# The two stores of each group of v cover exactly the partitions that hold needed rows

## The reference, cut to what matters

```python
def _L1_gnn_ref(x, spatial_encoding, edge_encoding, Wq, Wk, Wv, Wo):
    n, d = x.shape                      # 3327, 128
    h = Wq.shape[0] // d                # 8
    q = (x @ Wq.T).reshape(d, n, h)
    k = (x @ Wk.T).reshape(d, n, h)
    v = (x @ Wv.T).reshape(d, n, h)
    a = jnp.einsum('dnh,dmh->dnm', q, k) * d ** (-0.5)
    a = jax.nn.softmax(a + spatial_encoding + edge_encoding, axis=2)
    out = jnp.einsum('dnm,dmh->dnh', a, v)
    return out.reshape(n, h * d) @ Wo.T
```

## Time and profile before

| what | us |
|---|---|
| median of three runs (11011.2 to 11017.62) | 11016.96 |
| the profiled execution | 11012.01 |
| its span from first to last instruction | 11010.2 |
| first store of the projection phase issued | 364.5 |
| first and last store of v issued | 388.1 and 596.6 |
| first DMA of the phase behind it issued | 605.3 |

### The profile page before, as it was taken

How to read it: one execution, slowest core, us unless ns; L and a number is a source line. 1 busy time by engine, 2 the same in 40 slices (tenths; PEclk the granted TensorE clock), 3 DMA queues, 4 the chain that set the end, 5 groups by cost and what they waited for, 6 DMA issues and landing times. The chain is left out here.

```text
span 11010.2 us, 306891 instructions
## 1 busy us (share of the span) xinstructions
PE 9969.5 (91%) x115286; PEld 4497.9 (41%) x115286; DVE 9811.3 (89%) x9374; ACT 10319.1 (94%) x7187; POOL 7991.1 (73%) x3346
## 2 busy tenths in 40 slices
PE   7769999999999999899999999998999999999988
PEld 7435533333333333333333333333333333333383
DVE  6669999999999999899999999998999999999958
ACT  6569999999999999999999999999999999999916
POOL 0048888888888888788888888887888888888800
PEclk9979999999999999999999999999999999999999
DMA  9887743333333333433323332334323333333264
GB/s 404 277 192 100 100 80 49 48 49 50 49 48 49 50 49 48 94 50 50 49 47 50 50 49 47 50 54 91 49 47 50 50 49 47 50 50 49 43 213 175
DMA packets 426704, 879.88 MB, mean 80 GB/s; under 512 B 86871, under 2 KB 349406, under 8 KB 381694
## 3 DMA queue, kind: packets, MB, share of 16 engines
q1 hardware_dynamic: 426588, 878.33, 40.1%
HBM read 722.35 MB, written 155.64 MB: 80 GB/s over the span
## 5 line engine op out<-in xcount | busy, mean ns | idle before, releaser
L1287 DVE SCALAR_TENSOR_TENSOR a_probs<-ps,adj_ring 128x1024 f32<-128x1024 f32 x7488 | 8859.1, 1220 | 752.0 <-PE ps L1175 630.1
L1259 POOL TENSOR_TENSOR a_pool_probs<-a_pool_probs,adj_ring 128x1024 f32<-128x1024 f32 x3328 | 7974.7, 2396 | 1861.1 <-ACT a_pool_probs L1245 1861.1
L1248 ACT ACTIVATE a_probs<-a_probs 128x2048 f32<-128x2048 f32 (+1 forms) x3328 | 8698.6, 2614 | 27.6 <-DVE a_probs L1287 27.2
L1245 ACT ACTIVATE a_pool_probs<-ps 128x1024 f32<-128x1024 f32 x3328 | 5008.3, 1505 | 44.6 <-PE ps L1175 44.3
L1175 PE MATMUL ps<-a_q,a_k 34*128 34x512 f32 (+1 forms) x21632 | 4087.6, 445 | 793.6 <-ACT a_pool_probs L1245 613.2
L1195 PE MATMUL ps<-a_probs,a_v 128*9 128x256 f32 x59904 | 3855.8, 380 | 0.0
L1175 PEld LDWEIGHTS ps<-a_q,a_k 34*128 34x128 f32 x21632 | 1792.1, 184 | 3463.4 <-ACT a_pool_probs L1245 1630.0
L1195 PEld LDWEIGHTS ps<-a_probs,a_v 128*9 128x9 f32 x59904 | 1578.5, 91 | 1598.6 <-issue 196.8
L1195 PE MATMUL ps<-a_pool_probs,a_v 128*9 128x256 f32 x26624 | 2065.6, 382 | 4.2 <-DMA a_v<-v_ext 2.7
L1195 PEld LDWEIGHTS ps<-a_pool_probs,a_v 128*9 128x9 f32 x26624 | 395.4, 88 | 974.7 <-issue 934.7
L682 POOL MEMSET v_rows<- 128x512 f32 x2 | 1.9, 1039 | 352.4 <-POOLq L94 352.4
(11 more groups left out here) (178 smaller groups left out, 2355.1 us busy)
## 6 DMA issues: line engine op xcount, KB each, us to landing
a_k<-k_parts SPq DMA_DIRECT2D x1664, 208.0 KB
a_q<-q_parts SPq DMA_DIRECT2D x3072, 16.0 KB
a_v<-v_ext SPq DMA_DIRECT2D x384, 117.0 KB, 2.1
adj_t<-tr SPq DMA_DIRECT2D x26, 1664.0 KB, 19.4
g2tile<-adj_t SPq DMA_DIRECT2D x26, 1664.0 KB, 7.1
nat<-in_adj SPq DMA_DIRECT2D x25, 1663.5 KB, 18.0
e_nat<-in_adj SPq DMA_DIRECT2D x25, 1663.5 KB, 6.9
adj_ring<-adj_t SPq DMA_DIRECT2D x54, 512.0 KB, 7.5
```

What stands on the lines that cost most here:

```text
L1245: nc.scalar.activation(probs(k), score(j), ACT.Exp, scale=SCALE).then_inc(scores_exped, 1)
L1248: nc.scalar.activation(sums_of(k), sums_of(k), ACT.Exp, scale=2.0).then_inc(sums_exped, 1)
L1259: nc.gpsimd.tensor_tensor(beside(c, probs(k)), beside(c, probs(k)), adj_of(c, j), ALU.mult).then_inc(multiplied, 1)
L1287: v.scalar_tensor_tensor(out=beside(c, probs(k)), in0=beside(c, score(j)), scalar=SCALE / 2, in1=adj_of(c, j), op0=ALU.mult, op1=ALU.add). ...
```

## The change

Two lines are replaced. For group g with columns `begin` to `end`, `upper` is now the number of partitions of the first store itself and `lower` the first partition of the second store itself. Before, the one was rounded up and the other down to a multiple of 16.

```diff
                     begin, end = v_groups[g]
-                    upper = min(P, -(-(P - begin // BLOCKS) // 16) * 16)
-                    lower = (P - end // BLOCKS) // 16 * 16
+                    upper = P - begin // BLOCKS
+                    lower = P - end // BLOCKS
                     sp.wait_ge(v_copied, HEADS * (g + 1))
                     sp.dma_start(v_ext[P:P + upper, begin:end], v_rows[g % 2][0:upper, 0:end - begin, :]
                                  ).then_inc(v_stored[g % 2], LOAD)
                     sp.dma_start(v_ext[lower:P, begin + 1:end + 1], v_rows[g % 2][lower:P, 0:end - begin, :]
                                  ).then_inc(v_stored[g % 2], LOAD)
```

## The result

| | before | changed |
|---|---|---|
| median of five runs | 11016.96 (11011.2 to 11018.31) | 11230.32 (11228.81 to 11239.62) |
| ratio | | 1.0195, 95% interval 1.0184 to 1.0206 |
| span of the profiled execution | 11010.2 | 11227.0 |
| projection phase, first store issued to first DMA behind it | 240.8 | 453.6 |

The kernel became 213 us slower while it stored 1.7 MB less. The slices show where, against the earlier trace rows: the second and third. The fourth to the sixth differ too, since work comes there that came 213 us sooner before.

A forecast was written before the change was run, and what follows sets the result against it. DMA engines bound the projection phase; on the fullest, 170.8 (q, k) + 275.8 (389 rows of v) + 3.2 (half rows) + 8 (landing, gaps) make 458 us, 217 over 240.8; on 11012 that is 11229 us, range 11180 to 11285.

The forecast's parts named there:

- The reading of three transfers: DMA dealing: equal shares over the most engines, up to sixteen, that the row count allows; read from 112, 15, 127 rows.
- SP's hold of 10.08 us: At the issue of the load of x: taken as a sign that its 127 rows lay on one engine.
- The share of 0.07 and the packets in single file: Load of x, 16.9 to 17.2 us: one engine of sixteen at work, 22 packets in 0.50 us, so 127 rows on one.
- The sum: Projection phase, fullest engine: 389 rows of v at 0.709 us plus q and k, 458 us in place of 240.8.
- The engine that never idles: Projection phase: the fullest engine's backlog covers the computing, the next group arriving some 5 us before it runs dry.
- Part 1: Stores of v at lines 623 and 625: 1.71 MB no longer stored gain 4 to 5 us if nothing else changes.
- the last rival: Whole kernel faster by over 22 us: no mechanism, as v's stores are 46 us per engine and lose 8% of bytes; 0.01.
- The 23.6 us left over: Phase before, 240.8 measured against 217.2 summed: landing, gaps and slower rows of v when sixteen engines store; 8 kept.
- Even dealing: Stores of v: rows dealt as evenly as the count allows, 0 us or 4 to 5 us gained, 11007 to 11012; chance 0.11.
- other engines: Stores of v: each one-engine store goes to another engine, 42 us fall away, 11187; chance 0.05.
- all on one: Stores of v: every count not a multiple of sixteen goes to one engine, 267 us on top, 11496; chance 0.06.
- the first rival: Stores of v dealt evenly, some engines one row more: 11007 to 11012, the change doing what its size suggests; chance 0.11.

The follow-up runs named there:

- e7_x_split: Kernel before, with the load of 127 rows of x taken as 112 and 15 rows, v's stores unchanged: 11021.02 us, ratio 1.0003.
- e6_split: Changed kernel's exact rows, each store cut into the largest multiple of 16 and a remainder in its own DMA: 11027.79 us, 1.0008 against the kernel before.
- e8_all_rows: Kernel before, with both stores of v covering all 128 partitions in every group: 11016.32 us, ratio 0.9998.
- e1: Kernel before, with only line 623 covering the exact counts, line 625 keeping multiples of 16: 129.6 us slower, ratio 1.0118.
- e2: Kernel before, with only line 625 covering the exact counts: 84.8 us slower, ratio 1.0077.
- e3: Kernel before, with only the stores of a prime count (109, 89, 19, 59) exact, the others multiples of 16: 165.5 us slower, ratio 1.0148.
- e5: Kernel before, with only group 1's row count at line 623 changed from 112: 109 rows 67.1 us slower, 122 34.4, 111 22.2, 110 5.1.

## Why the prediction was right

**The bound.** DMA bounds the phase: PE, DVE and ACT did the same busy time in both, and the phase grew by 212.8 of the 216.8 us of span.

**How rows are dealt.** The reading of three transfers (127 rows on one engine, 15 spread, 112 on sixteen) was confirmed: 109, 122, 111 and 110 in one place give 1, 2, 3 and 11 engines, primes and composites apart add up, and the rows under way show 13, 10, 14 and 3 engines for 39 and 78, 50, 98 and 69. The page of the Trainium skill named in the prediction (DMA: Bandwidth & Descriptors, "Why a DMA increments its semaphore by 16 and not by 1") gives the same rule, and the runs agree: shares of 0.06, 0.12 and 0.18 for one, two and three engines. That the engines used are the lowest-numbered is its statement; the runs show only that the 89 and the 59 rows share one.

One leg of the argument was wrong: SP's hold of 10.08 us at the load of x was given as a sign of the 127 rows. It stays with 112 rows (e7_x_split), so the count of 127 is not its cause; the load ahead is the likely one, not shown. The share of 0.07 and the packets in single file carried the step alone. Also, the 15 rows landed 1.7 us behind the 112 (10955.0 and 10953.3), not 1.3, which is the difference of the two durations; against the 7.5 us of work that 15 rows on one engine would be, it changes nothing.

**The sum.** Predicted for the phase 458 us, measured 453.6. A row alone on its engine took 0.69 us, not 0.709, 7 us less on 389 rows. The rest beside the packets: 453.6 - 170.8 - 389 x 0.69 - 3.2 = 11 us, where 8 was kept; 4 of the 11 are packets of q and k, which took 0.0495 us in place of 0.0483. The two misses offset each other in part. The median was forecast at 11229 and came at 11230.3, and that closeness is luck: it is 213 us over its own before, where 217 were forecast over a profiled execution 5 us below the median.

**The engine that never idles.** Right: the distances from group to group grew by 0.61 to 0.69 us per row more wherever 17 rows or more were added to the fullest engine, but for group 3 (9.4 us for 19 rows, 0.49), and compute hid nothing. Group 4 got 3.1 us faster with 50 and 98 rows in place of 64 and 112, on ten and fourteen engines: its rows took 0.93 us in the mean in place of 1.22.

**The bytes.** Part 1 was wrong as a term, without effect on the forecast. It priced 90 rows at 4 to 5 us "if nothing else changes". Storing the exact rows nearly evenly, with eleven DMAs more, was 10 us slower (e6_split), and storing 560 more cost nothing (e8_all_rows). The price took one rate for all rows, but rows of different stores have different rates. (Of the 19.3 MB of v, 1.71 are 9%, not the 8% of the last rival.)

**The 23.6 us left over.** The prediction put them down to landing, gaps and "rows of v that take longer when sixteen engines store at once". By the packets 19 of them are slow rows of v (62.6 us in place of 43.2) and 4 are packets of q and k at 0.0495 us in place of 0.0483; the packets overlap a little, which leaves room for landing and gaps. But the condition named is not the right one: in e8_all_rows sixteen engines store at once, and a row takes 0.71 us. It is stores of fewer than 128 partitions that have the slow rows. The forecast needed only that a row alone on its engine is not slow, and that held (0.69 us).

**The rivals.** Even dealing, other engines and all on one each failed at e1, e2, e3 or e5, by 20 us or more. The time that the first rival gave for the case that the change does what its size suggests, 11007 to 11012, was not reached either: with the rows spread by more DMAs it was 11028, 10 us above before. Spread rows without the added DMAs were not run.

**What would have shown it.** Predicted were a share of about 0.55 over the phase (0.50), stretches of some 75 and 100 us behind groups 1 and 2 (ACT's longest wait 98 us), and groups 3 and 4 nearly as before (9.4 us more, 3.1 less).

## What to carry to other kernels

Count a DMA's rows on its fullest engine before its bytes: with n rows, find the largest divisor of n up to 16 by trying 16, 15, 14 and so on (110 goes to 11 engines, which is easy to miss), and prefer a few unneeded rows to a prime count, or cut the transfer into a multiple of 16 and a rest. A row of 18 KB cost 0.64 to 0.74 us on the fullest engine here, and everything queued behind it on that engine waits with it, so 109 rows in place of 112 cost 67 us. When an issue is held, look at the transfers ahead of it first; when engines are busy, look at the rate too.

## What the runs showed of the hardware that was not expected

- Rows of 18 KB took an engine 0.71 us when both stores of a group covered all 128 partitions (windows of 413 to 422 GB/s) and 0.88 to 1.22 us in the mean when one or both covered fewer (windows of 223 to 340 GB/s, packets of q and k among them), at the same busy share of 1.0. 11.35 MB more were free (ratio 0.9998).
- A DMA of 89 rows on one engine, with 59 behind it on the same one, held SP not at its own issue (0.25 us) but at the three behind it: 15.31, 43.65 and 49.48 us.
- With compute idle for 30 us, TensorE's granted clock stood at 0.50 (1.2 GHz) in the stall, where the full level of 1.00 (2.4 GHz) stands in windows in which PE works, and the phase's mean fell from 0.87 to 0.70. PE was busy as long as before (154.2 and 154.6 us), under the DMA's work, so nothing of it shows in the time.
